# Products of the identity in TensorE's waits at stage boundaries of a twelve-stage kernel

## The reference

```
x = L0_attn_x
x = x + 0.5 * _L0_ffn_ref(_layernorm(x, axis=-1), L0_ffn_weight)      # x @ sign(W).T
x = x + _L0_attn_ref(_layernorm(x, axis=-1), ...)                     # softmax attention, 16 heads of 64
x = x + 0.5 * _L0_ffn_ref(...)
x = x + 0.5 * _L1_ffn_ref(...)                                        # 16 gated experts, top 2, and a shared one
x = x + _L1_attn_ref(...)                                             # 4 layers of a selective state space
x = x + 0.5 * _L1_ffn_ref(...)
x = x + 0.5 * _L2_ffn_ref(...)                                        # 16 GELU experts, top 4
x = x + _L2_attn_ref(...)                                             # linear and windowed attention, gated
x = x + 0.5 * _L2_ffn_ref(...)
x = x + 0.5 * _L3_ffn_ref(...)                                        # quantised weights with a low-rank part
x = x + _L3_attn_ref(...)                                             # attention with squared relu, 16 heads
x = x + 0.5 * _L3_ffn_ref(...)
return x
```

## Time and profile before

| | |
|---|---|
| median of three runs | 2634.88 us (2629.48 to 2635.0) |
| profiled execution | 2637.11 us, its span 2635.3 us |
| mean granted TensorE clock | 0.971 |
| TensorE busy (products) | 2467.8 us, 94% of the span, 11094 instructions |
| TensorE busy (weight loads) | 1405.0 us, 53% |
| VectorE busy | 1934.5 us, 73%, 3923 instructions |
| ScalarE busy | 1616.5 us, 61%, 3503 instructions |
| GpSimd busy | 1148.1 us, 44%, 924 instructions |

### The profile page before, as it was taken

One profiled execution on the slowest core, in us unless ns is written; L12 is line 12 of the kernel. 1 busy time (PEld: TensorE's weight loads), 2 busy tenths in 40 slices (PEclk: granted clock), 3 DMA queues, 4 the chain that ended last, 5 costly groups with the idle time before them and its releaser, 6 DMA issues. The chain is left out here.

```text
span 2635.3 us, 37625 instructions
## 1 busy us (share of the span) xinstructions
PE 2467.8 (94%) x11094; PEld 1405.0 (53%) x11094; DVE 1934.5 (73%) x3923; ACT 1616.5 (61%) x3503; POOL 1148.1 (44%) x924
## 2 busy tenths in 40 slices
PE   7999989899999999999989999988879998799988
PEld 5767754455555555555444444466644444456655
DVE  7888867799999999999966445466634444577754
ACT  4565533688888888888833344477744443466644
POOL 1000012599999999999930002022200001355442
PEclk8999989999999999999999999999989998999998
DMA  2000024344444444444443221000011110000000
GB/s 110 1 1 1 0 89 94 119 161 161 163 164 159 164 161 164 160 166 157 167 141 82 79 99 65 0 2 1 1 49 65 65 65 28 1 1 1 1 1 17
DMA packets 34771, 205.70 MB, mean 78 GB/s; under 512 B 4016, under 2 KB 5168, under 8 KB 13360
## 3 DMA queue, kind: packets, MB, share of 16 engines
q1 hardware_dynamic: 34608, 203.83, 22.0%
HBM read 201.19 MB, written 2.62 MB: 77 GB/s over the span
## 5 line engine op out<-in xcount | busy, mean ns | idle before, releaser
L1520 POOL TENSOR_TENSOR mam_state_c<-mam_state,weights_r 128x1024 f32<-128x1024 f32 x256 | 600.3, 2365 | 10.1 <-DVE mam_state L1482 8.3
L1482 DVE TENSOR_TENSOR_SCAN mam_state<-banks,mam_dbu 128x1024 f32<-128x1024 f32 x256 | 577.1, 2275 | 1.6 <-ACT banks L1551 0.7
L1601 PE MATMUL banks<-mam_state_c,identity 128*128 128x512 f32 x1024 | 485.0, 606 | 10.6 <-POOL mam_state_c L1520 9.8
L1551 ACT ACTIVATE banks<-mam_dt,mam_a_neg 128x255 f32<-128x255 f32 x1024 | 425.0, 461 | 63.7 <-DVE mam_state L1482 63.2
L1601 PEld LDWEIGHTS banks<-mam_state_c,identity 128*128 128x128 f32 x1024 | 187.2, 190 | 224.1 <-issue 189.2
L1027 PE MATMUL banks<-route_xnt,weights_r 128*128 128x512 f32 x512 | 243.3, 598 | 1.9 <-PEq L736 1.0
L1465 DVE TENSOR_TENSOR mam_dbu<-banks,weights_r 128x1024 f32<-128x1024 f32 x192 | 227.5, 1198 | 0.0
L434 ACT ACTIVATE at_probs<-banks,at_nmax 128x256 f32<-128x256 f32 x256 | 117.9, 473 | 139.1 <-DVE at_nmax L375 139.1
L556 POOL TENSOR_SCALAR route_ln_rs<-route_ln_mv 128x4 f32<-128x4 f32 x16 | 5.1, 318 | 449.3 <-DVE route_ln_mv L634 449.3
L2710 POOL TENSOR_TENSOR at_attention<-at_relu 128x512 f32<-128x512 f32 x128 | 131.2, 1042 | 127.4 <-ACT at_relu L2755 79.7
L975 DVE TENSOR_TENSOR m2b_hidden<-m2b_gelu,m2b_comb_spread 128x512 f32<-128x512 f32 x120 | 80.7, 690 | 116.4 <-ACT m2b_gelu L1005 113.8
(11 more groups left out here) (433 smaller groups left out, 5012.3 us busy)
## 6 DMA issues: line engine op xcount, KB each, us to landing
weights_r<-mam_bc_rows SPq DMA_DIRECT2D x128, 1024.0 KB, 4.7
m2a_comb_spread<-m2a_comb_rows SPq DMA_DIRECT2D x15, 1024.0 KB, 8.0
m2b_comb_spread<-m2b_comb_rows SPq DMA_DIRECT2D x15, 1024.0 KB, 8.0
m1a_comb_spread<-m1a_comb_rows SPq DMA_DIRECT2D x14, 512.0 KB, 6.9
m1b_comb_spread<-m1b_comb_rows SPq DMA_DIRECT2D x14, 512.0 KB, 7.5
weights_r<-in_mb SPq DMA_DIRECT2D x1, 4332.0 KB, 12.9
weights_r<-in_m SPq DMA_DIRECT2D x1, 4200.0 KB, 12.8
weights_r<-in_a SPq DMA_DIRECT2D x1, 2632.0 KB, 10.7
```

Source lines behind the costliest of these rows:

```text
L1482: dve.tensor_tensor_scan(flat2(h[:, i % 4, :, :, :]), decay(i), flat2(dbu[:, i % 4, :, :, :]), 0.0, ALU.mult, ALU.add).then_inc(h_ready, 1)
L1520: pool.tensor_tensor(hc[:, j % 4, :, :, :], h[:, j % 4, :, :, :], c_rows(j), ALU.mult).then_inc(hc_ready, 1)
L1551: i = act.activation(decay(j)[:, o + 1:o + S], dt[:, q, c, 1:S], ACT.Exp, scale=aneg[:, l, k:k + 1])
L1601: k = pe.matmul(y_bank(q)[:, :], K.ident[:, :], flat(hc[:, j % 4, n, :, :]), start=(j == 0 and n == 0), stop=(j == NP - 1 and n == 1))
```

## The change

A helper issues n products of the identity with itself into one bank, with no semaphore. It is called at these places of TensorE's program:

```
+def idle_products(K, pe, bank, n):
+    for k in range(n):
+        pe.matmul(K.ps[bank][:, (k % 4) * P:(k % 4 + 1) * P], K.ident[:, :], K.ident[:, :], start=True, stop=True)
...
 def stage_signed_ffn(K, tag):            # f0a, f0b
+                pe.wait_ge(K.consts_ready, K.N_CONST)
+                idle_products(K, pe, 7, 10 if first else 7)
                 for n in range(B + 1):
...
                         i.then_inc(prod, 1)
+                idle_products(K, pe, 0, 10 if ahead else 4)
                 if ahead:
                     route_tensor(K, ahead, pe, 0, "xt")
+                    idle_products(K, pe, 0, 3)
...
+                idle_products(K, pe, 7, 10)              # at0
                 transposed_input(0, 1)
                 pe.wait_ge(xnt_ready, 1)
                 project(0, 0, 0)
                 values(0, 0, 0)
+                idle_products(K, pe, 2, 6)
                 over_sequences(pe, slot, G, TAIL)
...
                         if p and e == 2:                 # m1a, m1b
+                            if M and p == NP:
+                                idle_products(K, pe, 6, 6)
                             pe.wait_ge(yt_ready, p)
...
+                if M:
+                    idle_products(K, pe, 6, 9)
...
                         if p and e == 1:                 # m2a, m2b
+                            if p == NP:
+                                idle_products(K, pe, 0, 3)
                             pe.wait_ge(yt_ready, p)
...
+                idle_products(K, pe, 0, 4)
...
                         if i == 12:                      # at2
+                            if not now:
+                                idle_products(K, pe, 4, 10)
                             pe.wait_ge(ot_ready, s + 1)
...
                             k.then_inc(y_ps, 1)
+                            if not now:
+                                idle_products(K, pe, 4, 4)
...
                         k.then_inc(o_ps, 1)              # f3a, f3b
+                if first:
+                    idle_products(K, pe, 5, 3)
...
                 pe.wait_ge(K.consts_ready, K.N_CONST)    # at3
+                idle_products(K, pe, 0, 14)
                 pe.wait_ge(K.loaded["a3"], 16)
...
                         else:
+                            if first and n == 2:
+                                idle_products(K, pe, 0, 9)
                             pe.wait_ge(silu_ready, s * 4 + n - 1)
...
                     if last and i == 9:
                         s, q = last
+                        if not now:
+                            idle_products(K, pe, 0, 12)
                         pe.wait_ge(fac_ready, s + 1)
...
                         k.then_inc(y_ps, 1)
+                        if not now:
+                            idle_products(K, pe, 0, 4)
```

More of the change, by code:

```diff
@@ L531, in slot @@
                         k.then_inc(av_ps, 1)
+                idle_products(K, pe, 7, 10)
                 transposed_input(0, 1)
```

## The result

The changed kernel took 2619.48 us (median of 5 runs, 2619.24 to 2620.91) against 2634.88 (5 runs, 2629.48 to 2635.0) for the kernel before: ratio 0.9949, 95% interval 0.9937 to 0.996. That is faster, by 15.4 us, where 11.05 were forecast. The profiled execution took 2619.48 us with a span of 2617.8, against 2637.11 and 2635.3.

The account below looks back on a forecast made before the run. TensorE's clock, halved behind waits at stage boundaries, was taken to cost time on the chain; savings of 12.8 us less costs of 1.75 gave 11.05, from 2634.88 to 2623.8 us (predicted 2624; 8 in 10: 2616 to 2633).

Parts of the forecast that it names:

- The price: Everywhere: one added identity product takes 0.24 us at the full clock, twice that at the half clock.
- The stage ends: Ends of f0a, at2 and at3: four products delay the barrier, 0.45 us each, 1.35 in all.
- The first ten: Start of the first stage: ten products at the half clock delay the first transposes; cost 0.3 us, bounds 0 and 1.5.
- at3's start: Start of the last attention: 1.1 us saved in the first low-clock stretch and 1.5 in the second.
- its tail: at3's tail: two groups of eight instructions speed up, 2 x 1.79 us, less 0.3 for VectorE's operations; 3.3 us saved.
- m2b's start: Start of m2b: eight instructions taking 5.06 us run at the full clock; 1.3 us saved of at most 1.4.
- m1a: Start of the first experts: logits and weight transposes speed up about 0.45 us each; 0.9 saved, at most 3.4.
- at0: Start of the first attention: projections and values 1.8, first slot 1.8, transposes and next slot 0.5; 4.1 us saved.
- No effect on the clock: Rival, whole kernel: filling doesn't keep the clock up, only costs of 6.6 us stay, 2641.5 us; chance 0.09.
- Others set the pace: Rival, whole kernel: clock stays up but half of each saving is absorbed, net 4.65 us, 2630.2; chance 0.15.
- More is won: Rival, whole kernel: falls inside stages may vanish too, 5 to 8 us more, 2616 to 2619; chance 0.10.
- The price of 0.31: Rival, all filled places: each product takes 0.31 us, costs 4.5 in place of 1.75, 2626.6 us; counted inside the forecast.

Follow-up runs that it names:

- the narrow one: Changed kernel with the moving operand and output of the filling products cut from 128 to 16 columns; 2640.13 us, ratio 1.0022 against the kernel before.
- the last run: Changed kernel with one more full identity product behind each of the three 16-row products at m2a's start; 2624.37 us, ratio 0.996 against the kernel before.

## Why the prediction was right, and where it was off

**The sign and the mechanism were right.** Filling keeps the clock up, and the clock is what brings the time: 16 columns in place of 128 take the gain away and leave the costs. Each mark that the prediction named is in the rows above: clock 1.00 from 20 to 35 us, 3.67 at m2b for 3.6, 1.99 twice in the tail, 5.55 us there for 5.8, eight filling instructions in 1.06 us for 0.95, the first stage's end not moved. Of the span 75.2 us moved from 0.50 to 1.00, where 55 were forecast; 58 of them are the stretches at the filled places, all of which are gone.

**The price** was 0.25 us (0.24 forecast). **The stage ends** cost 0.40 and 0.41 us at f0a and at3 (0.45 forecast) and about 0.3 at at2. **The first ten** cost nothing (0.3 forecast): they take 4.37 us and the first transposes come at 7.73 in place of 6.78, but f0a's last addition to x starts at 18.44, 0.13 us earlier than before. VectorE had worked ahead, and the 0.95 us were made up within the stage.

**The gains were sized too small**, 12.8 in the sum; with the costs taken out they came to 17.2 at the filled places. At at3's start (2.6 forecast, 3.1 measured) and in its tail (3.3 and 3.6, the measured one without the stage end) the terms stand. Three are off:
- m2b's start: 1.3 forecast, 3.3 measured (3.0 and the 0.3 of the stage end). The step took only the eight instructions in the first fallen stretch. A second one followed at 1974.02 to 1977.43 in the kernel before; it is gone too, and VectorE's lag changes by 1.3 at the first and by 1.7 at the second. A fall was costed by one window, where a place had two.
- f0b 0.6 forecast and 0.9 measured, m1a 0.9 and 1.6. In m1a VectorE's lag changes by 0.3 at the logits, and by 0.6 and 0.4 at the first hidden products and the next statistics, which the step had left to VectorE and the table load.
- at0: 4.1 forecast, 4.7 measured (4.3 and 0.4).

With these the filled places give 16.3 us in place of 11.15. The medians differ by 15.4, the profiled executions by 17.5. The step that failed is "I take what lies on the chain" for these three; it cut too much.

**The rivals.** No effect on the clock: refuted by the changed kernel, and realised by the narrow one, within 1.4 us of its worked-out time. Others set the pace, 2630.2: refuted, since at at0's start and at3's tail nearly the whole saving arrived. More is won, 2616 to 2619: the result, 2619.48, lies between it and the forecast; its reason, stretches inside stages that vanish or come new, is seen in the lower half of the table with both signs, -1.3 in sum, so it was the places' own sizes that gave more and not this. The price of 0.31: refuted.

**What stays open.** Why the clock falls inside m1b, m2a, at2, f3a and f3b in some executions and not in others of nearly the same program. At m2a's start it fell in eight of thirteen traces before the last run. Two attempts there and one in at2 brought no time. Half the filling everywhere but at m2b and at3's start may do as well as the changed kernel; it wasn't run, and the spread of the runs wouldn't show a difference under 2 us.

## What to carry to other kernels

Where the granted clock halves behind a wait at a stage boundary and the next work of TensorE is a link of the chain, useless full-width products in the wait can win back nearly all of what the low clock cost there (3.6 us in at3's tail, the whole of 2 x 1.79), and the places add up. Fill the wait short of its end: half the filling kept most of the gain (11 of 15 us), twice the filling turned it into a loss of 12 us. Before filling, look at what follows: where a fall only moves from a wait onto dense work, as in the quantised stages, it costs more than it brings.

## What was unexpected of the hardware

- A product with 16 moving columns occupies TensorE nearly as long as one with 128: eight instructions at the end of at3 took 0.96 us in the narrow kernel and 1.06 in the changed one. It doesn't hold the clock, 0.50 with TensorE busy 16.54 of 17.06 us. So the busy time of the profile didn't tell here whether the clock stays.
- Transposes of the identity held the clock as products did (0.987 mean clock).
- Identity against identity, nearly all zeros, held it too (1.00 from 20 to 35 us), which no row of before had shown.
- The clock fell also with no idle time ahead: in the kernel with m1b's end filled too it was granted 0.50 from 1458.11, and TensorE had been busy without a gap since 1452.13, the last part of it with products of 16 rows.
